# Second layer's attention: V blocks of 512 queries behind the second score group, in place of two halves of 256 queries

## The reference

```python
scores = einsum('bhsd,bhtd->bhst', q, k) * SCALE;  attn = softmax(scores);  ctx = einsum('bhst,bhtd->bhsd', attn, v)
output = lin(merge_heads(ctx), Wo, bo)
rq = split_heads(lin(output, Wrq, brq));  rk, rv = (split_heads(lin(past_states, ...)) ...)
rattn = softmax(einsum('bhsd,pbhtd->pbhst', rq, rk) * SCALE);  rctx = einsum('pbhst,pbhtd->pbhsd', rattn, rv)
recursive_output = merge_heads(rctx).mean(axis=0)      # then a sigmoid gate blends output and recursive_output
```

## Time and profile before

| | |
|---|---|
| median of 3 runs | 945.72 us (940.9 to 945.82) |
| profiled execution, span | 953.6 us |
| PE busy | 876.9 us (92%) |
| DVE busy | 747.2 us (78%) |
| ACT busy | 586.4 us (62%) |
| POOL busy | 279.4 us (29%) |
| V products of layer 1 | about 367 to 803 us |

### The profile page before, as it was taken

One profiled execution on the slowest core, in us unless ns is written; L12 is line 12 of the kernel. 1 busy time (PEld: TensorE's weight loads), 2 busy tenths in 40 slices (PEclk: granted clock), 3 DMA queues, 4 the chain that ended last, 5 costly groups with the idle time before them and its releaser, 6 DMA issues.

```text
span 953.6 us, 19265 instructions
## 1 busy us (share of the span) xinstructions
PE 876.9 (92%) x6883; PEld 550.2 (58%) x6883; DVE 747.2 (78%) x2162; ACT 586.4 (62%) x1277; POOL 279.4 (29%) x419
## 2 busy tenths in 40 slices
PE   8899999988888899999999999999999989888994
PEld 7456566555478775444444534454443434888994
DVE  6888888877456677988989798978997893785674
ACT  2457575655656426798889877877766775332431
POOL 6123233435411445403210111001025313244332
PEclk9799999998979998999999999999987897988997
DMA  4325310001102114700000000000251100102123
GB/s 133 104 58 139 107 45 24 20 23 37 42 15 81 48 37 144 235 1 2 2 1 2 1 2 1 1 2 1 79 193 40 24 1 24 35 26 74 46 60 115
DMA packets 47928, 48.38 MB, mean 51 GB/s; under 512 B 5607, under 2 KB 39399, under 8 KB 47577
## 3 DMA queue, kind: packets, MB, share of 16 engines
q1 hardware_dynamic: 39784, 38.03, 13.8%
q0 software_dynamic: 3296, 6.82, 2.3%
q10 hardware_dynamic: 4752, 2.30, 0.8%
HBM read 30.83 MB, written 21.02 MB: 54 GB/s over the span
## 4 chain that ended last, share of the span: by engine, by line
PE 66%; DVE 24%; issue 3%; ACT 2%; POOL 2%; another core or an unknown queue 1%; DMA 1%; DVEq 0%; POOLq 0%; ACTq 0%; SPq 0%
PE pv L1726 15%; PE st L1703 9%; PE ring L1694 9%; DVE M L2026 6%; PE ring L1595 6%; PE ring L1840 5%; PE st L1595 4%; DVE ring L2030 3%; PE st L1825 3%; PE ring L1656 2%; PE ring L1606 2%; DVE M L2033 2%; PE st L1833 2%; PE st L1818 2%; PE pv L1833 1%
## 5 line engine op out<-in xcount | busy, mean ns | idle before, releaser
L1452 ACT ACTIVATE Et<-st 128x512 f32<-128x512 f32 (+3 forms) x768 | 373.7, 550 | 130.4 <-PE st L1703 122.5
L2033 DVE TENSOR_REDUCE M<-ring 128x1 f32<-128x512 f32 x256 | 160.4, 683 | 29.3 <-PE ring L1694 28.8
L2026 DVE TENSOR_REDUCE M<-ring 128x2 f32<-128x512 f32 x256 | 159.7, 682 | 16.3 <-PE ring L1694 15.4
L2030 DVE CUSTOM_DVE_ANT_0 ring<-ring,maskw 128x128 f32<-128x128 f32 (+3 forms) x256 | 121.8, 511 | 26.4 <-PE ring L1694 24.9
L1726 PE MATMUL pv<-Et,Va 128*32 128x256 f32 (+3 forms) x1536 | 136.8, 418 | 1.6 <-POOL Et L1266 1.6
L1694 PE MATMUL ring<-Kbd,Qa 128*128 128x128 f32 (+3 forms) x256 | 91.4, 382 | 10.3 <-DVE M L2030 7.3
L1266 POOL TENSOR_SCALAR_AFFINE_SELECT Et<-Et 128x256 f32<-128x256 f32 x128 | 54.3, 426 | 141.1 <-ACT Et L1452 139.6
L1726 PE MATMUL pv<-Et,RV 128*32 128x256 f32 x1024 | 90.0, 422 | 0.7 <-ACT PVs L1459 0.5
L1703 PE MATMUL st<-Qb,Kbd 128*128 128x512 f32 (+3 forms) x256 | 85.7, 355 | 3.9 <-ACT Et L1452 3.8
L1694 PE MATMUL ring<-RKT,Qa 32*128 32x512 f32 x256 | 78.9, 528 | 7.2 <-DVE M L2026 5.7
L1703 PE MATMUL st<-Qb,RKT 32*128 32x512 f32 x256 | 78.5, 532 | 1.7 <-ACT Et L1452 1.2
(11 more groups left out here) (293 smaller groups left out, 1535.9 us busy)
## 6 DMA issues: line engine op xcount, KB each, us to landing
Xd<-Xd SPq DMA_DIRECT2D x8, 1056.0 KB, 16.5
L1W<-in_L1W SPq DMA_DIRECT2D x2, 2048.0 KB, 12.2
Kbd<-Ksb SPq DMA_DIRECT2D x60, 64.0 KB, 2.0
Xs<-Xd SPq DMA_DIRECT2D x39, 66.0 KB
W<-in_L0W SPq DMA_DIRECT2D x8, 258.0 KB, 3.8
W<-in_L0W SPq DMA_DIRECT2D x8, 256.0 KB, 4.2
G<-Zd SPq DMA_DIRECT2D x8, 256.0 KB, 3.2
Yd<-Yt ACTq DMA_DIRECT2D x30, 64.0 KB
```

Of the source, the lines that this page charges most:

```text
L1452: e.activation(Et[s // 2 % 4][:, j % 2, q0:512], bank(ph)[:, q0:512], ACT.Exp, scale=SCALE).then_inc(exp_done, 1)
L2026: e.tensor_reduce(M[i][:, t, j, :], bank(ph)[:, :].rearrange("p (two n) -> p two n", two=2), AX.X, ALU.max).then_inc(mx_red, 1)
L2030: e.tensor_tensor_reduce(bank(ph)[:, 0:n], bank(ph)[:, 0:n], maskw[:, 512 - n:512], 1.0, -3e38, ALU.add, ALU.max, M[i][:, t, j, 0:1]).then ...
L2033: e.tensor_reduce(M[i][:, t, j, 0:1], bank(ph)[:, 0:n], AX.X, ALU.max).then_inc(mx_red, 1)
```

## The change

In layer 1 the step `pva` is gone. `pv` of chunk c - 1 multiplies all 512 queries and stands where it stood, behind the second pair of scores; the step where `pva` was is empty. The number of steps is the same, and so is the place of every other step. Layer 0 has only `pv` before and after.

```diff
@@ -239,10 +239,7 @@
                 continue
             do("st", l, u, c, 0)
             do("st", l, u, c, 1)
-            yield
-            if c:
-                do("pva", l, u, c - 1)
-            yield
+            yield from wait(2)
             do("st", l, u, c, 2)
             do("st", l, u, c, 3)
             yield
@@ -251,7 +248,6 @@
             yield
         yield from wait((3, 1)[l])
         if l:
-            do("pva", l, u, 3)
             yield from wait(2 if u < 31 else 0)
         do("pv", l, u, 3)
         if ends_sum(unit):
@@ -1702,11 +1698,11 @@
-                elif what in ("pva", "pv"):
+                elif what == "pv":
                     l, u, c = a
                     kind, k, b, g = units[l][u]
                     rec = kind == "rec"
-                    cols = slice(128 * c, 512) if l == 0 else slice(0, 256) if what == "pva" else slice(256, 512)
+                    cols = slice(128 * c if l == 0 else 0, 512)
@@ -1724,8 +1720,8 @@
                         ins = nc.tensor.matmul(pv[32 * j:32 * j + 32, cols], v, Et[s // 2 % 4][:, j % 2, cols],
-                                               start=first and (l == 0 or what == "pva"), stop=done, skip_group_check=True)
-                        if j % 2 and what == "pv":
+                                               start=first, stop=done, skip_group_check=True)
+                        if j % 2:
                             ins.then_inc(pv_half, 1)
```

## The result

| | before | after |
|---|---|---|
| median | 945.77 us (4 runs, 940.9 to 950.15) | 970.76 us (4 runs, 963.67 to 975.23) |
| ratio | | 1.0292, 95% interval 1.0248 to 1.0336 |
| profiled execution, span | 953.6 us | 961.9 us |
| PE, DVE, ACT busy | 876.9, 747.2, 586.4 us | 864.5, 747.8, 584.4 us |

The change makes the kernel 25 us slower; 19 were forecast. The two profiled executions are only 8.3 us apart, and that says little: the stage that the change touches, from layer 1's first score to its last V product, takes 440.3 us before (362.9 to 803.2) and 467.6 after (353.7 to 821.3), 27.3 more, while the first layer and the experts behind were 9.2 and 9.8 us shorter in this execution, at a higher granted clock (0.98 and 0.94 against 0.94 and 0.90). So what follows compares the stage, and its parts.

What follows compares the result with a forecast made beforehand. PE was taken to set the pace for most of the stage, VectorE the rest. Longer chunks add 27.6 us, up to 15.2 given back; +19 taken, scaled to +18.8 on 945.7: 964.5 us, range 943 to 982.

Steps and rivals of the forecast that it cites:

- 1.19 from score 0 to score 3: Second-layer scores: score 3 reuses score 0's bank, so it cannot start before 1.17 to 1.19 us after score 0.
- the whole block: One V product block of 512 queries on PE: 1.00 us, against 1.14 for two halves; 18 us less work over 128.
- the quiet chunk: Second-layer chunk with nothing else between its score groups: 2.62 us against 2.17 to 2.19, +0.43 each.
- the chunk with the keys' transposition: Next keys transposed between the score groups, taking the third score bank: 3.71 us against 3.31, +0.40.
- the rule of X + 1.43: Chunks where score 3 waits for a later ScalarE exponential: old time X + 1.00, new time X + 1.43.
- The one with the normalisation: Chunk with the normalisation's transposition between score groups: changes by -0.40 + 0.43, plus at most 0.1 for the Qb transposition.
- the give-back: Chunks where the old kernel waited for something else, such as VectorE's reduces: up to 0.5 each, 15.2 us at most.
- The positives: Sum over the second-layer chunks counted as longer, 61 of 124 by over 0.3: 27.6 us.
- VectorE decides: Rival: VectorE's work ends last nearly everywhere in the stage, so time stays the same, 943 to 950 us; chance 0.14.
- PE's work decides: Rival: part 1's saved block work, 18 us, comes out: 928 us, or 937 for half of it; chance 0.12.
- The clock falls as well: Rival: PE's idle time lowers the clock, adding 10 to 15 us: 975 to 980 us; chance 0.14.
- Chunks with projections between their groups: Chunks with 1.79 us of transposition and projection between score groups: the wait is hidden and each gains 0.14.

Runs made afterwards that it cites:

- dvehalf pair: VectorE's second-layer maxima taken over half the keys: kernel before 928.09 us (0.9697), changed kernel 958.1 us (1.0013), both against the kernel before.
- halves_behind: Changed kernel with two half blocks in place of the whole one, both behind the second score group: 989.95 us, 1.0363 of the kernel before.
- whole_between: Changed kernel with the whole block moved between the two score groups: 967.76 us, 1.0121 of the kernel before.
- 128 pads of 0.64 us: Changed kernel with two unused 128x128 products ahead of score 2 in each second-layer chunk: 1003.79 us, 1.048 of the kernel before.

## Why the prediction was right, point by point

- **The terms.** The main ones came true: 1.19 from score 0 to score 3 measured 1.17; the whole block 1.00 measured 0.99 to 1.00; the quiet chunk 2.62 measured 2.60; the chunk with the keys' transposition 3.71 measured 3.75 (506.83 to 510.58 in the changed kernel). The chunk behind the queries' transposition lasted 2.60 before, so the rule of X + 1.43 gives 3.03; it measured 2.74, since score 3 could start 1.30 after score 0 there (1.61 before), ScalarE being less far behind with its copies. The one with the normalisation, 3.21 before, was to change by 0.03 to 0.13 and measured 3.45; its last maxima product started 0.26 behind the one beside it, which the sum had not. These four add to 12.6 to 12.7, and the unit measured 12.49 to 12.54: errors of -0.3 and of +0.1 to 0.2 that partly cancel.
- **Where the forecast was short.** The term that was mis-sized is the give-back. The positives added to 27.6 us, and I took them down to 19 because VectorE would work off its backlog while PE waits. The stage grew by 27.3 in the first profiled execution, at the upper end of the 12 to 28, and by 34.0 in the second, at a lower clock; the medians differ by 25 and 30. A give-back exists, 3.0 us of 18.4 between copies 3 and 19, as the dvehalf pair shows; the forecast took 8.6 of 27.6, about a third. Behind copy 19 (at 607 us of the kernel before) the stage grew by 10.7 (196.2 to 206.9). There the granted clock differs from execution to execution, down to 0.62 in single units, and the runs don't tell how much was given back.
- **VectorE decides (0.14).** Wrong for the quiet units, as the unchanged 11.28 shows. In units 15 and 23 it is nearly so: they grew by 0.2 only.
- **PE's work decides (0.12).** A visit to the column tiles costs 0.14 whatever is done in it, as halves_behind shows. The rule of the Trainium skill (TensorEngine Tiling, Key Properties) that a change of the tiling mode drains the engine agrees with this in kind. But whole_between, which saves the same visits, is 1.2% slower than the kernel before, and 128 pads of 0.64 us cost the changed kernel 19 us, not 73. The saved visits are there (14.16 for 15.60 in unit 5 holds some of them); in quiet chunks they only lengthen a wait.
- **The clock falls as well (0.14).** Not borne out as a cause: at equal mean clock the kernels are as far apart, and the quiet units differ at full clock. As an addition it is open. The changed stage had a mean clock of 0.96 and 0.93 in its two profiled executions, the one of before 0.94, and 0.96 and 0.93 are 6.7 us apart with equal quiet units. Unit 24 alone took 19.68 us in both, at 0.64 and 0.65, against 14.85 at 0.89 before; with half reduces, at full clock, it took 12.94 against 12.16. Units 26 and 27 behind it were together 6.4 us shorter than before in the one execution and 1.5 in the other. So the clock can hide or add several us in any one execution, and the difference between the ratios on two chips (1.029 and 1.031) says nothing further.
- **Chunks with projections between their groups** were to gain 0.14. Two around 480 us, with projections in both gaps, gained 0.03 and 0.36 (5.60 to 5.57, 4.44 to 4.08).

## What to carry to other kernels

With n buffers and producers issued in clumps, look at the (n+1)th product: it needs the buffer of the first. The time from the first one's start to that buffer's release (here 1.17 to 1.19 us) must be filled with work that stands between the two in the producer's queue. Half a block there was worth more than the 0.14 us that joining the halves saves, and which gap needs it depends on what the schedule already puts there, chunk by chunk. Busy shares of 82 to 98% on three engines don't mean that one covers for another: from copy 3 to copy 19, VectorE's work hid 3.0 us of 18.4, in the units that it set itself, and nothing in the quiet ones.

## What the runs showed of the hardware

- The fixed cost of a group of column-tiled products, 0.14 us, comes once for each run of them between other tilings: 16 records of 256 columns in a row took 1.00 us, 8 of 512 also 1.00.
- A row-tiled group right behind another row-tiled one starts 0.34 us after it (504.23 to 504.57), and a V block starts 0.43 to 0.44 after a row-tiled group (505.40 to 505.84).
- A score product of 512 columns and its exponential on ScalarE take 1.17 us until the product that needs the bank starts (504.23 to 505.40), and 1.18 where three scores were issued in a row (523.32 to 524.50). Four exponentials in a row took 2.06 us.
